# A graph network on one core: extra, unused matrix products in the stage that builds the adjacency tiles

## The chip, the cores and the metric

The kernel runs on one core of one Trainium2 chip. The metric is the device time of that core in microseconds (us): the median of the runs of the kernel before is 6002.23 us, of three runs from 5999.04 to 6010.08 us. Less is better.

## The reference, cut to what matters

The reference is a network of four graph layers on 6250 nodes with 64 features and 200,000 edges, sorted by destination: a two-round gated message layer, a graph convolution, a mean aggregation with edge features, and an edge network followed by a gated unit. The sums over edges that the first three need are all of this kind:

```
msg_in = jnp.concatenate([hv[dst], hv[src], e], axis=1)
msgs = msg_in @ W_msg[t] + b_msg[t]
a = jax.ops.segment_sum(msgs, dst, num_segments=num_nodes)
...
out = jax.ops.segment_sum(msgs, dst, num_segments=n_nodes)      # convolution
agg = jax.ops.segment_sum(x_j, col, num_segments=N)             # mean
```

A sum over edges of rows of the source nodes is a product with the adjacency matrix (how many edges go from source s to destination d). The kernel builds that matrix once and multiplies with it several times. Only the building is touched here.

## The kernel before, in words

**The building.** The 6250 nodes are cut into 49 tiles of 128 (`NT`). A destination tile is cut into 16 windows of 8 destination nodes (`WT`, `DW`). For each window the result is a matrix of 128 (position of the source in its tile) by 392 (49 source tiles by 8 destinations), held in one PSUM bank; four banks are used in turn (`bank_w`: two halves of `ps_zz`, `ps_t`, `ps_a`). The edges lie in chunks of 128, one edge to a partition; since they are sorted by destination, a window needs a run of chunks, taken two at a time (`GW`): a *group*. Each window has a first group and, in a loop, as many *further groups* as its edges need (`more`). The destinations are drawn so that small node numbers have most edges: the first tile has 108 further groups in its 16 windows, the last ones have none.

**Who does what.** For each group VectorE makes two one-hot operands: the position of the source (`oh_lo`, L1555) and the pair of source tile and destination (`oh_hi`, L1557), and then signals `s_wsem`. TensorE waits for it (L1125), multiplies the two chunks' operands into the bank (two MATMULs of 392 columns, L1127) and with the second gives the operand buffer back (`s_woh`). There are four buffers for first groups, one per bank, and two for further groups: `rest = GF + k % 2`, one for even windows and one for odd. So a second further group of a window is written only when TensorE has read the first. When a window's groups are done TensorE closes the bank with a product of one column (L1135), signals `s_win`, and ScalarE copies the bank as fp8 into the tile (L800) and frees it (`s_winf`). After each tile ScalarE makes the keys of the tile after the next one (L789, L790), and SyncE stores the finished tile to DRAM.

**Order.** All order is that in which the code is written; there is no planner. TensorE's loop runs over 49 tiles with 16 windows written out, with a loop over further groups in each. VectorE's and ScalarE's loops take two tiles a turn. At each tile's start TensorE and VectorE load the tile's counts into registers (L421). After the 49 tiles TensorE transposes an auxiliary matrix and goes on to the first product with the adjacency.

**Unused products elsewhere.** The gated units already have such a thing: `WARM = 16` products of `ident_h` with itself, 128 columns each, written into `ps_a` and never read (L997).

Of the kernel before, what the change touches and what calls it, by code (L numbers as in the profile page):

```python
# [22 lines left out]
P = 128  # L23
# [55 lines left out]
def gnn(nc, D, out):  # L79
    with ExitStack() as ctx:  # L80
        def sb(name, shape, dt=f32):
            return ctx.enter_context(nc.sbuf_tensor(name, shape, dt))

        def ps(name, shape):
            return ctx.enter_context(nc.psum_tensor(name, shape, f32))
# [60 lines left out]
        ident_h = sb("ident_h", [P, P], bf16)  # L146
# [118 lines left out]
        ps_acc = ps("ps_acc", [P, 512])  # L265
# [153 lines left out]
        def load_windows(eng, t, first):  # L419

            _, vals = nc.values_load_multi_w_load_instructions(  # L421
                win_tab[0:1, ds(t, 1), first:2, :].rearrange("o t a w -> o (t a w)"), engines=[eng.engine],
                min_val=0, max_val=CH, skip_runtime_bounds_check_because="chunk numbers and counts")
            lim = [(0, CH - 1), (0, GWMAX - 1)][first:]
            vals = [nc.s_assert_within(r, *lim[k // WT], skip_runtime_bounds_check_because="the search bounds it")
                    for k, r in enumerate(vals)]
            return [(k % GF, GF + k % 2, k, *vals[k::WT]) for k in range(WT)]

        def load_range(eng, t, which=(0, 1)):

            lim = [(0, CH - 1), (1, GMAX), (0, NT * GMAX), (1, SMAX), (1, RBMAX), (1, RBG), (0, CH - 1)]
            k0, k1 = which[0], which[-1] + 1
            _, vals = nc.values_load_multi_w_load_instructions(
                tile_tab[0:1, ds(t, 1), k0:k1].rearrange("o w a -> o (w a)"), engines=[eng.engine],
                min_val=0, max_val=NT * GMAX, skip_runtime_bounds_check_because="chunk numbers and counts")
            return [nc.s_assert_within(vals[k - k0], *lim[k], skip_runtime_bounds_check_because="the search bounds it")
                    for k in which]
# [126 lines left out]
        def _(pool):  # L564
# [26 lines left out]
            with pool.Fori(0, NT) as t:  # L591
                lo, _, _, ng = load_range(pool, t, (0, 1, 2, 3))
                with pool.Fori(0, ng) as g:
                    c = first_chunk(pool, lo, g, 2 * SC, CH - 1)
                    for b in range(2):
                        features = e16a[:, ds(c + b * SC, SC), :]
                        pool.wait_ge(s_e3f, 1)
                        pool.sem_inc(s_e3f, -1)
                        pool.tensor_tensor(eparts[:, b, 1, :, :], features, upper(features), ALU.subtract).then_inc(s_pool, 1)  # L599
                        pool.wait_ge(s_pool, 1)  # L600
                        pool.sem_inc(s_pool, -1)
                        pool.tensor_tensor(eparts[:, b, 2, :, :], eparts[:, b, 1, :, :], eparts_h[:, b, 1, :, :],
                                           ALU.subtract).then_inc(s_e3, 1)
# [287 lines left out]
        def _(pe):  # L891
# [223 lines left out]
            def build_tile(t):  # L1115

                if True:
                    for i, rest, _, more in load_windows(pe, t, 1):
                        pe.wait_ge(s_winf[i], 1)
                        pe.sem_inc(s_winf[i], -1)  # L1120

                        def group(first):
                            u = i if first else rest
                            pe.wait_ge(s_wsem, 1)
                            pe.sem_inc(s_wsem, -1)  # L1125
                            for j in range(GW):
                                m = pe.matmul(bank_w[i][:, 0:WC], oh_lo[u][:, :, j], oh_hi[:, u, j, :],  # L1127
                                              start=first and j == 0, stop=False)
                            m.then_inc(s_woh[u], 1)

                        group(True)
                        with pe.If(more):
                            with pe.Fori(0, more):
                                group(False)
                        pe.matmul(bank_w[i][:, 0:1], zrow_h[0:1, 0:P], zrow_h[:, 0:1], start=False,  # L1135
                                  stop=True).then_inc(s_win, 1)


            pe.wait_ge(s_cst2, 1)
            pe.sem_inc(s_cst2, -1)  # L1140
# [33 lines left out]
            for k in range(3):  # L1174
# [3 lines left out]
                          stop=True).then_inc(s_wc, 1)  # L1178
# [4 lines left out]
            with pe.Fori(0, NT) as t:  # L1183
                build_tile(t)
# [756 lines left out]
```

## Time and profile before

| what | value |
| --- | --- |
| median of three runs | 6002.23 us (5999.04 to 6010.08) |
| profiled execution | 5999.94 us, of which the span is 5998.2 us |
| mean granted TensorE clock over the span | 0.717 |
| building the adjacency | 818.7 to 2131.7 us of the span, 1313.0 us |
| in it: TensorE busy | 873.60 us |
| in it: VectorE busy | 745.99 us |
| in it: ScalarE busy | 576.84 us |

"Granted clock" is the mean of TensorE's clock over a stretch as a share of full speed: it has two levels here, 1.0 (2.4 GHz) and 0.5 (1.2 GHz), and a value between them says how much of the stretch was at each. A matrix product's busy time contains the time that it needs to drain, so products that follow each other overlap in it and a busy TensorE is not one at its peak. The three stretches used below are tiles 0 to 4 (818.7 to 1239.2 us), tiles 5 to 27 (to 1778.1 us) and tiles 28 to 48 (to 2131.7 us).

### The profile page before, as it was taken

To read this page: it belongs to the slowest core of one execution; us is meant where nothing else is said; L and a number is where in the kernel's file an instruction comes from. 1 tells how busy PE (TensorE), PEld (TensorE's weight loads), DVE (VectorE), ACT (ScalarE), POOL (GpSimd) and SP (SyncE) were. 2 spreads that over 40 slices of the span, in tenths; PEclk is the share of its full clock that TensorE was granted. 3 is DMA by queue.
4 is the path that set the end of the run, shared out by engine and by line. 5 is a ranking of instruction groups with operands and counts; after the bars stand their busy time and mean duration, and the time that the engine had idled before them with its cause. 6 is when DMAs were issued, how large, how long until landed. Compare 5 with 4: busy or idle time off the path is not lost. (4 is left out here: it accounts for less than half of the span.)

```text
span 5998.2 us, 125746 instructions
## 1 busy us (share of the span) xinstructions
PE 3920.0 (65%) x29847; PEld 2606.8 (43%) x29848; DVE 3033.9 (51%) x8943; ACT 1290.4 (22%) x3582; POOL 2274.8 (38%) x2798
## 2 busy tenths in 40 slices
PE   0455325667677779797998985666666666666666
PEld 0344201122222258787988873333333333333335
DVE  4444753466666555333123225555555555555554
ACT  0222100144556730121000111111111111111112
POOL 0455560000000000211111016777777777777771
PEclk9999755588887789998999995555555555555557
DMA  3000000000001135132544433333333333333330
GB/s 128 0 0 0 1 2 6 11 29 32 39 39 50 50 133 179 44 134 103 176 156 176 140 109 84 91 88 88 89 88 88 88 87 87 87 87 87 86 85 23
DMA packets 220192, 460.12 MB, mean 77 GB/s; under 512 B 59440, under 2 KB 116796, under 8 KB 219357
## 3 DMA queue, kind: packets, MB, share of 16 engines
q1 hardware_dynamic: 163325, 401.37, 19.9%
q0 software_dynamic: 56672, 56.94, 5.3%
q14 instruction: 169, 1.38, 0.1%
q8 instruction: 26, 0.43, 0.0%
HBM read 415.43 MB, written 42.67 MB: 76 GB/s over the span
## 5 line engine op out<-in xcount | busy, mean ns | idle before, releaser
L676 POOL DMA_INDIRECT scr<-ptable,idx_st x1722 | 1668.8, 969 | 589.0 <-issue 439.5
L644 POOL COPY late<-late 128x256 f32<-128x256 f32 (+1 forms) x65 | 25.3, 390 | 2500.5 <-POOLq L642 2500.5
L937 PE MATMUL ps_zz<-sb_w_e,late 64*128 64x128 f32 x1148 | 439.6, 485 | 399.8 <-PEq L936 384.5
L1018 PE MATMUL ps_zz<-scr,arena 128*128 128x192 bf16 x7203 | 616.9, 248 | 65.1 <-PEq L1016 65.1
L1018 PEld LDWEIGHTS ps_zz<-scr,arena 128*128 128x128 fp8e4 x7203 | 605.3, 99 | 75.6 <-issue 72.9
L868 ACT COPY idx_st<-src_i 128x2 int32 x864 | 166.0, 192 | 1921.2 <-ACTq L874 1921.2
L937 PEld LDWEIGHTS ps_zz<-sb_w_e,late 64*128 64x128 f32 x1148 | 286.1, 308 | 577.5 <-issue 573.2
L950 PE MATMUL ps_acc<-scr,onehot 128*128 128x192 bf16 x1722 | 414.1, 341 | 162.8 <-PEq L948 144.7
L1557 DVE TENSOR_TENSOR arena<-arena 128x196 int32 x1323 | 470.2, 355 | 0.2 <-issue 0.2
L1127 PE MATMUL ps_zz<-arena,cand 128*128 128x392 fp8e4 x784 | 249.0, 408 | 337.5 <-PEq L1125 334.5
L1335 DVE TENSOR_TENSOR scr<-scr 128x128 f32<-128x128 f32 x861 | 253.8, 295 | 408.8 <-DVEq L1334 400.5
L1018 PE MATMUL ps_zz<-arena 128*128 128x192 bf16 x4802 | 406.1, 247 | 25.1 <-PEq L1016 25.1
L1018 PEld LDWEIGHTS ps_zz<-arena 128*128 128x128 fp8e4 x4802 | 400.2, 98 | 29.4 <-issue 28.1
L1441 DVE TENSOR_REDUCE arena<-ps_zz 128x64 f32<-128x192 f32 x196 | 70.1, 358 | 636.1 <-DVEq L1439 636.0
L937 PE MATMUL ps_t<-sb_w_e,late 64*128 64x128 f32 x574 | 219.1, 483 | 261.7 <-PEq L936 220.5
L1318 DVE TENSOR_TENSOR onehot<-dst_s,itile 128x256 bf16<-128x256 int16 x861 | 367.5, 427 | 6.2
L1312 DVE TENSOR_SCALAR late<-scr,tcol 128x256 bf16 x861 | 315.8, 367 | 41.5 <-DVEq L1311 31.6
L1327 DVE TENSOR_TENSOR scr<-ps_zz,scr 128x128 f32<-128x128 f32 x574 | 167.0, 291 | 315.9 <-DMA scr<-ptable,idx_st 228.5
L1555 DVE TENSOR_TENSOR scr<-scr,late 128x256 bf16<-128x256 f16 x539 | 157.5, 292 | 312.7 <-DVEq L1554 229.7
L937 PEld LDWEIGHTS ps_t<-sb_w_e,late 64*128 64x128 f32 x574 | 143.1, 308 | 349.5 <-issue 344.5
L940 PE MATMUL ps_zz<-arena,late 128*128 x3444 | 288.2, 240 | 0.0
L599 POOL TENSOR_TENSOR eparts<-arena 128x102 f32 x310 | 160.3, 517 | 325.2 <-DVEq L1700 172.6
(335 smaller groups left out, 5971.0 us busy)
## 6 DMA issues: line engine op xcount, KB each, us to landing
arena<-a_dram SPq DMA_DIRECT2D x245, 784.0 KB, 4.3
scr<-in_dst_lin SPq DMA_DIRECT2D x287, 384.0 KB
a_dram<-arena SPq DMA_DIRECT2D x49, 784.0 KB, 3.3
scr<-ptable,idx_st POOLq DMA_INDIRECT x1722
late<-in_e32c SPq DMA_DIRECT2D x861, 32.0 KB
arena<-in_e16p SPq DMA_DIRECT2D x1, 13387.5 KB, 34.7
h<-mm_dram SPq DMA_DIRECT2D x2, 832.0 KB, 5.3
x<-in_x_nm SPq DMA_DIRECT2D x1, 1664.0 KB, 7.0
```

The source lines that it names most:

```text
L676: pool.indirect_dma_start(grow[:, j, :], None, ptable, bass.IndirectOffsetOnAxis(ap=idx_st[:, j:j + 1], axis=0)).then_inc(s_row[j], 16)
L868: act.copy(idx_st[:, 2 * b:2 * b + 2], src_i[:, ds(c + 2 * b, 2)]).then_inc(s_ix, 1)
L937: pe.matmul(z, e32t[:, b, :], W["w_e3"][:, :], start=True, stop=False).then_inc(s_etf[b], 1)
L940: m = pe.matmul(z[:, i * H:(i + 1) * H], onehotT[:, b, i * P:(i + 1) * P], qsp[:, ds(t, 1), p * H:(p + 1) * H], start=False, stop=i == 1 a ...
L950: m = pe.matmul(ps_acc[:, 0:3 * H], onehot[:, j, :], msg_h[:, j, :, :], start=False, stop=False)
L1018: last = pe.matmul(ps_z[b % 2][:, 0:3 * H], amat[b][:, i, :], hsp[k % 2][:, i, :], start=(i == 0), stop=(i == NT - 1))
L1127: m = pe.matmul(bank_w[i][:, 0:WC], oh_lo[u][:, :, j], oh_hi[:, u, j, :], start=first and j == 0, stop=False)
L1312: v.tensor_scalar(onehotT[:, b, :], dstb[:, ds(r, 1), b, :], tcol[:, ds(t, 1)], None, ALU.is_equal).then_inc(s_ohT, 1)
L1318: v.tensor_tensor(onehot[:, 2 * b:2 * b + 2, :], bc(dst_s[:, ds(c + 2 * b, 2)], P), itile[:, :].unsqueeze(1).broadcast_to([P, 2, P]), ALU. ...
L1327: v.tensor_tensor(pre[:, 2 * b:2 * b + 2, :], bank_z[b][:, 0:2 * H].rearrange("p (j f) -> p j f", j=2), grow[:, 2 * b:2 * b + 2, :], ALU.a ...
L1335: v.tensor_tensor(msg[:, j, 1, :], msg[:, j, 0, :], msg_h[:, j, 0, :], ALU.subtract).then_inc(s_v, 1)
L1557: v.tensor_tensor(oh_hi_i[:, u, :, :, :], src_hot[:, ds(c, GW), :].unsqueeze(3).broadcast_to([P, GW, NT, 2]), dst_word[:, ds(c, GW), :].un ...
```

## The change

Behind each further group TensorE makes one product that nobody reads, and behind each closing of a window two. The product has 384 columns: `ident_h`, a bf16 identity of 128 by 128, times three copies of itself, into the bank `ps_acc`, which nothing else uses in this stage. It waits for nothing and signals nothing. The signals of the further group (`s_woh`) and of the closing (`s_win`) stand on the instructions before it.

```diff
                             m.then_inc(s_woh[u], 1)
+                            if not first:
+                                idle_product()
 
                         group(True)
                         with pe.If(more):
...
                         pe.matmul(bank_w[i][:, 0:1], zrow_h[0:1, 0:P], zrow_h[:, 0:1], start=False,
                                   stop=True).then_inc(s_win, 1)
-
+                        for n in range(2):
+                            idle_product()
+
+            def idle_product():
+                pe.matmul(ps_acc[:, 0:3 * P], ident_h[:, :], ident_h[:, :].unsqueeze(1).broadcast_to([P, 3, P]),
+                          start=True, stop=True)
```

TensorE's instructions for the first window of a tile, and the start of the second, before. `cand` and `scr` are the first and the further group's `oh_lo`, `arena` their `oh_hi`, `zrow_h` the closing's row of zeros; the rows between the branches run once per further group:

```order
L1127 MATMUL ps_zz<-arena,cand 128x392 [waits s_winf0,s_wsem]
L1127 MATMUL ps_zz<-arena,cand 128x392
L1132 COMPARE_AND_BRANCH
L1133 UNCONDITIONAL_BRANCH
L1127 MATMUL ps_zz<-arena,scr 128x392 [waits s_wsem]
L1127 MATMUL ps_zz<-arena,scr 128x392
L1133 REGISTER_ALU
L1133 COMPARE_AND_BRANCH
L1132 UNCONDITIONAL_BRANCH
L1135 MATMUL ps_zz<-zrow_h 128x1
L1127 MATMUL ps_zz<-arena,cand 128x392 [waits s_winf1,s_wsem]
```

The next window's first product follows the closing directly. The same place now:

```order
L1127 MATMUL ps_zz<-arena,cand 128x392 [waits s_winf0,s_wsem]
L1127 MATMUL ps_zz<-arena,cand 128x392
L1134 COMPARE_AND_BRANCH
L1135 UNCONDITIONAL_BRANCH
L1127 MATMUL ps_zz<-arena,scr 128x392 [waits s_wsem]
L1127 MATMUL ps_zz<-arena,scr 128x392
L1143 MATMUL ps_acc<-ident_h 128x384
L1135 REGISTER_ALU
L1135 COMPARE_AND_BRANCH
L1134 UNCONDITIONAL_BRANCH
L1137 MATMUL ps_zz<-zrow_h 128x1
L1143 MATMUL ps_acc<-ident_h 128x384 x2
```

One product has come into the loop over further groups, behind the product that frees the buffer, and two stand between the closing (now L1137) and the next window's first group. On the other engines no instruction moves.

## Rows read from the trace of the kernel before

**Rows 1.** Windows, all engines, the building in three stretches: busy time (instructions), then granted clock.
```profile
core 0: us, PE busy (x) PEld busy (x) DVE busy (x) ACT busy (x) POOL busy (x), PEclk, DMA share, GB/s
818.70:1239.20 420.50, 236.76 (x696) 55.26 (x696) 172.86 (x614) 56.43 (x89) 25.04 (x27) 0.53 0.03 9
1239.20:1778.10 538.90, 376.59 (x1632) 121.85 (x1632) 355.86 (x1264) 275.05 (x414) 0.00 (x0) 0.84 0.09 35
1778.10:2131.70 353.60, 260.25 (x1102) 83.52 (x1102) 217.26 (x769) 245.36 (x378) 0.00 (x0) 0.74 0.12 49
```

**Rows 2.** Windows, the same stretches, only the closings of L1135.
```profile
818.70:1239.20 420.50, 14.28 (x80) 7.75 (x80) 0.53 0.03 9
1239.20:1778.10 538.90, 63.88 (x368) 33.87 (x368) 0.84 0.09 35
1778.10:2131.70 353.60, 58.93 (x336) 31.50 (x336) 0.74 0.12 49
```

**Rows 3.** Timeline, tile 0, a chain of further groups: start, duration, engine, line, idle before.
```profile
1001.16 0.29 DVE L1555 TENSOR_TENSOR scr<-scr,late 128x256 bf16<-128x256 f16 x1 [1.54 <-DVEq L1554]
...
1001.88 0.81 PE L1127 MATMUL ps_zz<-arena,scr 128*128 128x392 fp8e4 x2 [1.08 <-PEq L1125]
1003.05 0.29 DVE L1555 TENSOR_TENSOR scr<-scr,late 128x256 bf16<-128x256 f16 x1 [1.32 <-DVEq L1554]
```

**Rows 4.** Timeline, tile 0, where one window ends and the next begins.
```profile
1010.20 0.18 PE L1135 MATMUL ps_t<-zrow_h 1*128 1x1 bf16 x1
...
1010.31 0.83 PE L1127 MATMUL ps_a<-arena,dif 128*128 128x392 fp8e4 x2
...
1010.94 0.86 PE L1127 MATMUL ps_a<-arena,scr 128*128 128x392 fp8e4 x2
1012.16 0.29 DVE L1555 TENSOR_TENSOR scr<-scr,late 128x256 bf16<-128x256 f16 x1 [1.55 <-DVEq L1554]
```

**Rows 5.** Timeline, tile 38, windows with one group each, low clock.
```profile
1961.62 0.83 PE L1127 MATMUL ps_zz<-arena,cand 128*128 128x392 fp8e4 x2
...
1962.39 0.18 PE L1135 MATMUL ps_zz<-zrow_h 1*128 1x1 bf16 x1
...
1962.50 0.83 PE L1127 MATMUL ps_t<-arena,dif 128*128 128x392 fp8e4 x2
```

**Rows 6.** Timeline, the same tile 8 us later, high clock.
```profile
1970.19 0.51 PE L1127 MATMUL ps_t<-arena,dif 128*128 128x392 fp8e4 x2
...
1970.63 0.17 PE L1135 MATMUL ps_t<-zrow_h 1*128 1x1 bf16 x1
...
1970.73 0.51 PE L1127 MATMUL ps_a<-arena,dif 128*128 128x392 fp8e4 x2
```

**Rows 7.** Line L997: duration min/median/max in ns, first and last start.
```profile
L997 PE MATMUL ps_a<-ident_h x384: 217/219/219, 2401.1 to 5983.6; 128*128 128x128 bf16 x192
```

**Rows 8.** Timeline, the last gated unit, products of L997 and their weight loads.
```profile
5909.70 0.65 PEld L997 LDWEIGHTS ps_a<-ident_h 128*128 128x128 bf16 x9
5909.86 0.61 PE L997 MATMUL ps_a<-ident_h 128*128 128x128 bf16 x8
```

**Rows 9.** Timeline, VectorE at the start of a tile, a first group, a further one, a first one.
```profile
1505.05 0.29 DVE L1555 TENSOR_TENSOR cand<-scr,late 128x256 bf16<-128x256 f16 x1 [2.36 <-DVEq L1554]
...
1505.90 0.29 DVE L1555 TENSOR_TENSOR scr<-scr,late 128x256 bf16<-128x256 f16 x1 [0.29 <-issue]
...
1506.50 0.29 DVE L1555 TENSOR_TENSOR cand<-scr,late 128x256 bf16<-128x256 f16 x1
```

**Rows 10.** Timeline, from the end of tile 37 to the start of tile 38.
```profile
1954.67 0.50 ACT L800 ACTIVATE arena<-ps_a 128x392 fp8e4<-128x392 f32 x1
...
1957.62 2.11 ACT L790 ACTIVATE late<-x,neg_base 128x1663 f16<-128x1663 f32 x1
1960.06 0.29 DVE L1555 TENSOR_TENSOR cand<-scr,late 128x256 bf16<-128x256 f16 x1 [6.26 <-DVEq L1554]
```

**Rows 11.** Windows, the first 3.5 us of TensorE's work in the tile of rows 9.
```profile
1505.70:1509.20 3.50, 3.36 (x11) 0.96 (x12) 2.70 (x10) 3.03 (x3) 0.00 (x0) 0.52 0.39 160
```

## The prediction, made before the change was run

> **What bounds the kernel now.** I read the windows view first, the building cut into three stretches [rows 1]. It is 1313.0 of 5998.2 us, and nothing outside it is touched, so all of the prediction is here. The reader should see that no engine is full: TensorE is busy 56%, 70% and 74% of the three stretches, VectorE 41%, 66% and 61%, ScalarE 13%, 51% and 69%. And TensorE's granted clock is 0.53, 0.84 and 0.74: in the first five tiles it is nearly always at the low level, though TensorE is busy more than half the time.
>
> Then the counts. The closings are 80, 368 and 336 [rows 2], 16 to a tile: 5, 23 and 21 tiles. Taken off the 696, 1632 and 1102 products of [rows 1] they leave 616, 1264 and 766 products of L1127, two to a group: 308, 632 and 383 groups, of which 228, 264 and 47 are further ones. So the change adds 2 x 784 + 539 = 2107 products.
>
> Last the timeline, for what each stretch waits on.
> - *Tiles 0 to 4: a chain through one buffer.* A further group's operands are written at 1001.16, multiplied from 1001.88 to 1002.69, and the next ones are written at 1003.05 [rows 3]: 1.89 us a group at the low clock, with TensorE idle 1.08 us of it.
> - *Tiles 5 to 27: VectorE.* It takes 0.85 us from a first group to a further one and 0.60 us from any group to the next first one [rows 9]. A tile has 16 windows and 264 / 23 = 11.5 further groups: 16 x 0.60 + 11.5 x 0.85 = 19.4 us. At the tile's start it stands 2.36 us [rows 9] or, at its loop's turn every second tile, 6.26 us [rows 10], 4.3 on average. Sum 23.7 us; measured 538.9 / 23 = 23.4. So VectorE's own pace explains this stretch.
> - *Tiles 28 to 48: VectorE and TensorE in turn.* VectorE's sum is 9.6 + 2.2 x 0.85 + 4.3 = 15.8 us a tile, measured 353.6 / 21 = 16.8. TensorE needs 0.88 us a window at the low clock (1961.62 to 1962.50) [rows 5] and 0.54 at the high (1970.19 to 1970.73) [rows 6], so at the low clock it is the slower one.
>
> **What a product costs.** Eight products of 128 columns with the same `ident_h` take 0.61 us, of which the last one's own duration is 0.219 [rows 7, 8]: (0.61 - 0.219) / 7 = 0.056 us each. Three times that is 0.17 us for 384 columns at the high clock. The pair of 392 columns says the same: 0.51 at high against 0.83 at low [rows 5, 6], a difference of 0.32 us in 784 columns, which makes 0.16 us a product at high and 0.33 at low. Two products behind a closing: 0.33 us high, 0.65 us low. Weight loads: nine of them take 0.65 us beside the eight products [rows 8], so they hide behind these; the first, behind the one-column closing, is exposed, but in its place the next window's first load goes behind the second product. A window with one group then costs TensorE 0.54 + 0.33 = 0.87 us at high and 0.88 + 0.65 = 1.53 at low, against VectorE's 0.60.
>
> The product behind a further group falls in the 1.08 us of idle time of [rows 3]: nobody waits. Cost 0 in a chain, and 0.16 us where TensorE is the bound. If the idle time were gone it would cost 0.16 to 0.33.
>
> **Tiles 0 to 4: +18 us.** At a window's turn the closing is at 1010.20, the first group at 1010.31, the further one at 1010.94, and VectorE goes on at 1012.16 when that one has been read [rows 4]. The two products stand between the first two of these, on the path: 80 x 0.65 = +52 us if the clock stays low. If it were always high they would cost 80 x 0.33 = 26, and the path would win back 0.32 us (0.83 against 0.51) in each of the 228 further groups, 73 us, and again in up to 80 first groups, 26: net -73. Those are the bounds. Between them decides how much of the time the clock is high. Now it is 6% (0.53). The products fill the turns of windows: 2 + 4 products of the groups + 1 in one piece, then the chain again with gaps of 0.7 us. The first tile has 108 further groups, in long chains where one product a group leaves TensorE idle for a third of the time; I expect the low clock there. In tiles 1 to 4, with one to three further groups a window, I expect high clock for half the time or more. Together some 33% high, 27 points more than now: 52 - 0.27 x 125 = +18.
>
> **Tiles 5 to 27: +17 us.** TensorE at the high clock: 16 x 0.87 + 11.5 x (0.33 + 0.16) = 19.5 us a tile. Its head is added. After tile 37's last closing ScalarE copies the bank at 1954.67, then makes keys until 1957.62 + 2.11 = 1959.73, and only then can it copy the next tile's first bank, 0.5 us [rows 10]: free at 5.9 us after the closing (0.3 us before the copy). TensorE fills four banks in 4 x 0.87 = 3.5 us and waits 2.4. Where VectorE's stand is 6.26 instead, its lead of four buffers covers 3.5 of it, which leaves about the same, 2.8. After such a pause the clock is low for a while, as now (0.52 in the first 3.5 us of a tile, after 2.36 us of standing) [rows 9, 11]: in 3.5 us two windows at 1.53 in place of 0.87, 1.3 to 2 us. Head 4.1 us; sum 23.6, as much as VectorE's 23.7. The mean is a tie, but the tiles differ. With 17 further groups VectorE's sum is 28.4 and TensorE's 26.3, no loss. With 5 they are 18.1 and 20.5: +2.4. Over the 23 tiles I take +0.75 a tile, +17. Bounds: 0, and +2.4 x 23 = +55.
>
> **Tiles 28 to 48: +47 us.** 13.9 + 2.2 x 0.49 + 4.1 = 19.1 us a tile on TensorE against 16.8 now: +2.25 x 21 = +47. Bounds: without the low clock after the head, 17.4, +13; with a head of 6 us, +87.
>
> **Sum.** 18 + 17 + 47 = +82 us. Against the profiled execution, 5999.94 us (span 5998.2 and 1.7 around it), that is 6082; the median of the runs is 2 us above the profiled one, so 6084 us, 1.4% slower. Where does the gain go? The clock rises in all three stretches, to about 0.65, 0.93 and 0.9, but only the first one waits for TensorE enough to be paid for it.
>
> **Rivals.**
> - *The clock pays (faster).* Products make the clock high throughout tiles 0 to 4 and at the tiles' heads. The place is the chain of [rows 3]; its price is up to -73 us, of which I take -45, since turns with one further group go at VectorE's 0.85 + 0.60 whatever the clock; then 0 in the middle and +11 late: about 5968 us. It decides once more than 42% of the first stretch's path is high (52 / 125) and the tile's head costs no low clock. For it: the added products raise TensorE's work in a chain by half. Against it: a chain even at high keeps TensorE idle for most of its 1.57 us, and today 0.56 busy [rows 1] gives 0.53 of clock. The Trainium skill, "TensorE: Matmul & The Clock Gate" (table "Why this matters for your kernels"), says that a matmul stream stays at full clock unless it has a long idle gap. By that rule this rival would hold. The trace disagrees: gaps of 1.08 us, and the low clock. Chance 0.06.
> - *The products are hidden (no change).* All three stretches have idle TensorE time, 183.7, 162.3 and 93.4 us [rows 1]. If the turns could absorb 784 x 0.33 = 259 us, the time stays at 6002. Against it: the late stretch has 93 us idle, and 336 x 0.33 = 111 go in. Chance 0.05.
> - *Products of an identity do not lift the clock (much slower).* Then real work is a smaller share of each stretch and the clock falls to low throughout: late 21 x (16 x 1.53 + 2.2 x 0.98 + 2.4) - 354 = +255; middle 23 x (24.5 + 11.5 x 0.98 + 2.4) - 539 = +339; early +52: 6650 us. No row separates it: L997's products stand among others. Chance 0.04.
> - *Each product's weight load is exposed.* 0.1 us more for each of two products in the windows where TensorE is the bound, the 336 late ones and half of the middle: 520 x 0.2 = +104, 6188 us. The Trainium skill, the same page (Part 2, the step on getting the stationary operand), lets the queue pull a load ahead of products in flight, which is this rival's denial; the trace agrees for L997 [rows 8], but not for the closing, 0.77 us after its group's start at the low clock where the two products need 0.65 [rows 5]. Chance 0.05.
>
> **How the numbers follow.** My forecast has 0.80. Its own range is 6035 to 6130: the early term from -15 to +45, the middle 0 to +35, the late +30 to +65, not all at one end. To leave out no more than 2 in 10 the range goes a little further, towards the exposed loads above and the clock that pays below: 6028 to 6140. A measurement of this kernel tells about 0.2%, 12 us, from no change. Slower by more: 0.80 less a little, + 0.04 + 0.05 = 0.88; the same 0.05; faster 0.07.
>
> **What would show it.** In the changed profile the building should end about 82 us later, with the late stretch some 19 us a tile, TensorE's idle time there ended by the free bank once a tile, and successive windows 0.87 us apart. The chain of tile 0 should keep 1.89 us at the low clock, and its turns be 0.65 us longer. The product's duration should follow 0.16 us start to start. Granted clock of about 0.65, 0.93, 0.9. If tile 0 shows a high clock, my early term is wrong and the sum falls; if late windows are 1.07 us apart, the loads are exposed; if the clock is 0.5 in all, products of an identity do not count.

## The result, and the profile after

The changed kernel takes 6078.76 us (median of four runs, 6074.57 to 6080.44) against 6000.64 us for the kernel before in the same comparison: a ratio of 1.0126, with a 95% interval from 1.0108 to 1.0143. The prediction was 6084 us, 82 us or 1.4% slower. Measured once more, beside the experiments of "Both, and the change once more" below, the ratio was 1.0134 (1.0118 to 1.0149).

The windows view of the changed kernel, the building in the same three stretches of tiles (0 to 4, 5 to 27, 28 to 48); columns as in [rows 1], then tile 0 and tiles 1 to 4 apart:

```profile
core 0: us, PE busy (x) PEld busy (x) DVE busy (x) ACT busy (x) POOL busy (x), PEclk, DMA share, GB/s
817.70:1249.30 431.60, 292.77 (x1084) 101.68 (x1084) 172.87 (x614) 56.37 (x89) 24.93 (x27) 0.68 0.03 8
1249.30:1814.50 565.20, 485.91 (x2633) 222.33 (x2632) 355.97 (x1264) 273.87 (x415) 0.00 (x0) 0.93 0.08 34
1814.50:2214.00 399.50, 342.50 (x1822) 150.62 (x1822) 217.64 (x770) 243.64 (x377) 0.00 (x0) 0.91 0.11 43
...
818.70:1026.00 207.30, 134.45 (x402) 40.42 (x400) 68.79 (x244) 7.75 (x16) 24.23 (x26) 0.57 0.01 1
1026.00:1249.30 223.30, 157.31 (x682) 61.03 (x680) 103.51 (x368) 47.99 (x73) 0.00 (x0) 0.79 0.04 15
```

The building ends at 2214 us in place of 2132 and everything behind it is as long as before. The stretches are +11, +26 and +46 us longer, and the clock rose in each: from 0.53 to 0.68, from 0.84 to 0.93, from 0.74 to 0.91. The clock did what such products can do, and the kernel got slower all the same. VectorE's busy time has not moved (172.87, 355.97, 217.64).

The line of the added product: count, and the shortest, median and longest duration in ns.

```profile
L1143 PE MATMUL ps_acc<-ident_h x2107: 323/326/528, 819.0 to 2213.9; 128*128 128x384 bf16 x192
```

It is the 2107 that were counted. What they do to successive windows stands in the timeline of tile 41, each window with one group, at the high clock:

```profile
2080.47 0.50 PE L1127 MATMUL ps_zz<-arena,cand 128*128 128x392 fp8e4 x2
...
2080.90 0.17 PE L1137 MATMUL ps_zz<-zrow_h 1*128 1x1 bf16 x1
2081.00 0.50 PE L1143 MATMUL ps_acc<-ident_h 128*128 128x384 bf16 x2
...
2081.23 0.29 DVE L1562 TENSOR_TENSOR cand<-scr,late 128x256 bf16<-128x256 f16 x1 [0.30 <-DVEq L1561]
2081.34 0.50 PE L1127 MATMUL ps_zz<-arena,cand 128*128 128x392 fp8e4 x2
```

Group, closing, two products, next group: 0.87 us, where [rows 6] had 0.54. TensorE's rows have no idle time before them: it waits for nobody. VectorE now waits for it: before its next first group it stands 0.30 us at L1561, where it waits for an operand buffer to be read. Over the late stretch its waits there before first groups grew from 110.5 to 161.9 us (the waits view of `cand` and `dif`). In tile 0 the turn of a window and the chains around it, with the start of VectorE's next operand:

```profile
1001.60 0.29 DVE L1562 TENSOR_TENSOR scr<-scr,late 128x256 bf16<-128x256 f16 x1 [1.32 <-DVEq L1561]
1002.31 0.81 PE L1127 MATMUL ps_zz<-arena,scr 128*128 128x392 fp8e4 x2 [0.76 <-PEq L1125]
1002.91 0.53 PE L1143 MATMUL ps_acc<-ident_h 128*128 128x384 bf16 x1
1003.49 0.29 DVE L1562 TENSOR_TENSOR scr<-scr,late 128x256 bf16<-128x256 f16 x1 [1.32 <-DVEq L1561]
...
1004.20 0.81 PE L1127 MATMUL ps_zz<-arena,scr 128*128 128x392 fp8e4 x2 [0.76 <-PEq L1125]
...
1004.81 0.52 PE L1143 MATMUL ps_acc<-ident_h 128*128 128x384 bf16 x1
1005.26 0.18 PE L1137 MATMUL ps_zz<-zrow_h 1*128 1x1 bf16 x1
1005.38 0.82 PE L1143 MATMUL ps_acc<-ident_h 128*128 128x384 bf16 x2
1005.99 0.86 PE L1127 MATMUL ps_zz<-arena,cand 128*128 128x392 fp8e4 x2
...
1007.87 0.29 DVE L1562 TENSOR_TENSOR scr<-scr,late 128x256 bf16<-128x256 f16 x1 [2.50 <-DVEq L1561]
1008.58 0.49 PE L1127 MATMUL ps_zz<-arena,scr 128*128 128x392 fp8e4 x2 [0.88 <-PEq L1125]
...
1009.44 0.29 DVE L1562 TENSOR_TENSOR scr<-scr,late 128x256 bf16<-128x256 f16 x1 [1.00 <-DVEq L1561]
```

The chain of [rows 3] still takes 1.89 us (1001.60 to 1003.49) with the product inside it: TensorE's idle time fell from 1.08 to 0.76 us, and the chain is no longer for it. The turn costs: from the last further group to the closing 1.06 us (1004.20 to 1005.26), from there to the next group 0.73 (to 1005.99) where [rows 4] had 0.11. Then, after the dense turn, the clock is high, and the next chain takes 1.57 us (1007.87 to 1009.44).

### The profile page after: what moved, and what is told of

The parts are those of the page before. It is cut to its first block and busy times, and to the rows that moved or that the text cites. A ratio compares the mean times of both kernels' runs of the same rounds, so it can differ in the third digit from the quotient of the medians.

```text
span 6078.6 us, 129960 instructions
## 1 busy us (share of the span) xinstructions
PE 4170.9 (69%) x31954; PEld 2821.8 (46%) x31955; DVE 3031.2 (50%) x8943; ACT 1287.2 (21%) x3582; POOL 2272.1 (37%) x2798
## 5 line engine op out<-in xcount | busy, mean ns | idle before, releaser
L1143 PE MATMUL ps_acc<-ident_h 128*128 128x384 bf16 x2107 | 621.2, 357 | 0.0
L1127 PE MATMUL ps_zz<-arena,cand 128*128 128x392 fp8e4 x784 | 216.6, 361 | 279.6 <-PEq L1125 279.6
```

The source lines that it names most:

```text
L1143: pe.matmul(ps_acc[:, 0:3 * P], ident_h[:, :], ident_h[:, :].unsqueeze(1).broadcast_to([P, 3, P]), start=True, stop=True)
```

## The experiments

All comparisons are with the kernel before on the same chip in the same call. Two things must be known to read them. The first four (each place alone, one column, three in chains) ran on one chip, on which the kernel before takes 6732 us, and the next three (tile ends, both, keys in the middle) on another, with 6739 us. On both the part behind the building is some 700 us longer and tile 0 some 25 us (see the last section); the other tiles of the building are as in the first comparison. I call these two the slower chips. The last four runs are from a third chip, where the kernel before takes 6005 us, about as in the first comparison (6001 us); which chip that one ran on is not on record. And the last stretch of the kernel before is 353.6 us in one profile and 359.9 in another [rows 1, and below], so a few us there say nothing. The three stretches of an experiment are given as its windows rows have them; the kernel before was not profiled on the slower chips, so as its first stretch there I take the 446 us of the run that leaves that stretch nearly alone (products at tile ends only). The times in us that go with a ratio are the ratio's difference from 1 times the kernel before.

### Each of the two places alone

```diff
-                        for n in range(2):
-                            idle_product()
```

> Only the product behind each further group stays, the two behind a closing go. Theory A (a product costs what it puts on TensorE's path, and the clock pays little): the product behind a window's last further group stands before the closing and the next first group, so the turns of tiles 0 to 4 get 0.33 us longer (26 us), the clock pays some of it back; the later tiles are VectorE's again. +5 to +20 us on before, late stretch within 3 us of the 353.6 before. Rival B (my prediction's sentence that a product in a chain costs nothing): 0, or faster by what the clock gives. Rival C (both kinds cost in proportion to their columns, 539 of 2107 products): +20 us.

Measured: ratio 1.0007 (0.9991 to 1.0024). Stretches 443.4, 545.0, 359.4 us, granted clock 0.64, 0.87, 0.76. So -3, +6 and 0 to +6: no change that can be told, -6 to +16 us by the interval, which holds rival B and most of theory A. The clock of the first stretch rose from 0.53 to 0.64 and paid little more than the turns took.

```diff
-                            if not first:
-                                idle_product()
```

> Only the two products behind each closing stay. Theory A: all of the late loss and most of the rest stays, +75 to +90 us on before: in tiles 28 to 48 TensorE still needs 0.87 us a window, in tiles 0 to 4 the turns still take 0.65 us more at the low clock, and the chains, without a product of their own, get less of the high clock than in the change (granted clock of the first stretch below 0.65), so the first stretch is longer than the 430.6 us of the change. Rival C (in proportion to columns, 1568 of 2107): +60 us.

Measured: ratio 1.0074 (1.0046 to 1.0102), 31 to 69 us. Windows view:

```profile
818.80:1271.70 452.90, 247.79 (x856) 72.72 (x856) 173.41 (x614) 56.36 (x89) 24.81 (x27) 0.64 0.02 8
1271.70:1827.20 555.50, 460.90 (x2369) 195.18 (x2368) 356.13 (x1264) 274.99 (x415) 0.00 (x0) 0.90 0.08 34
1827.20:2221.50 394.30, 335.32 (x1776) 146.10 (x1776) 217.81 (x770) 243.94 (x377) 0.00 (x0) 0.92 0.11 44
```

Against 446, 539 and 354 to 360 that is +7, +16 and +34 to +41. Most of the loss is that of the products behind the closings, and nearly all of the late one (394.3 of 399.5 us). The total is lower than the +75 to +90 that I expected. By the stretches the two places alone come to some 65 us against 80 of both, by the intervals to anything from 25 to 85, so whether they do more together than apart stays open.

### Instructions without columns

```diff
-                pe.matmul(ps_acc[:, 0:3 * P], ident_h[:, :], ident_h[:, :].unsqueeze(1).broadcast_to([P, 3, P]),
+                pe.matmul(ps_acc[:, 0:1], ident_h[:, :], ident_h[:, 0:1],
```

> The change with its products cut to one column: the same number of instructions and weight loads, no streaming. Theory A, where the clock follows the columns that are streamed and not the number of instructions: the clock falls below that of before, towards 0.5 in all three stretches, because each product's weight load (0.1 us) is now exposed and spreads the real columns out. TensorE then needs 0.88 + 0.21 = 1.1 us a window at the low clock: 21 x (17.6 + 3) late is +75, +50 to +100 in the middle, +30 early; +150 to +210 us. Rival D (instructions or weight loads keep the clock up, streaming is not needed): the clock stays as in the change, a window costs 0.54 + 0.2 = 0.75 us at high, under VectorE's pace at most tiles, and the kernel lands between before and +30 us.

Measured: ratio 1.0016 (0.9998 to 1.0034), -1 to +23 us. Windows view:

```profile
818.70:1268.00 449.30, 243.63 (x1084) 93.96 (x1084) 173.38 (x614) 56.33 (x89) 24.74 (x27) 0.53 0.02 8
1268.00:1810.10 542.10, 392.06 (x2632) 171.89 (x2632) 356.09 (x1264) 275.19 (x415) 0.00 (x0) 0.84 0.09 35
1810.10:2175.40 365.30, 287.07 (x1823) 108.75 (x1824) 217.79 (x770) 244.75 (x377) 0.00 (x0) 0.71 0.12 48
```

Its timeline, a late window with one group at the high clock:

```profile
1965.29 0.49 PE L1127 MATMUL ps_a<-arena,dif 128*128 128x392 fp8e4 x2
1965.72 0.17 PE L1137 MATMUL ps_a<-zrow_h 1*128 1x1 bf16 x1
1965.82 0.20 PE L1143 MATMUL ps_acc<-ident_h 128*128 128x1 bf16 x2
1965.88 0.49 PE L1127 MATMUL ps_zz<-arena,cand 128*128 128x392 fp8e4 x2
```

The same 2107 instructions and weight loads, and the clock is that of before: 0.53 and 0.84, and 0.71 in the late stretch, where the kernel before has 0.74 in one profile and 0.70 in another. So the instructions and loads alone do not raise it; with their 384 columns they do. Theory A had that right and the time wrong (+150 to +210 us, at a clock below that of before); the time is inside rival D's range, but D's clock, that of the change, is not there. I had each load cost 0.1 us; here a window takes 0.59 us (1965.29 to 1965.88) against 0.54 before, so two products with their loads cost 0.05 us once they have no columns. The late stretch is 5 to 12 us longer, and of the change's +46 the columns are the rest. With that the rival of the exposed weight loads is out.

### Where products cost nothing

```diff
                         with pe.If(more):
-                            with pe.Fori(0, more):
-                                group(False)
+                            with pe.If(pe.snap(more - 1)):
+                                with pe.Fori(1, more):
+                                    group(False)
+                                    for n in range(3):
+                                        idle_product()
+                            group(False)
```

> No product behind closings nor behind the last further group of a window; three behind each further group that another one follows (148 of them, where TensorE stands 1.08 us). Theory A: nothing is put on the path of a turn, three products take 0.99 us at the low clock and 0.5 at the high, both inside the 1.08 us, and the clock rises in tiles 0 to 4: chains at 1.57 in place of 1.89 us. First stretch 365 to 385 us in place of 420.5, the other two unchanged: -35 to -58 us on before. Rival E (what the further groups lose is their wait for VectorE, the clock cannot shorten the chain): 0. Rival F (three products reach into the next group's start): slower, a chain above 1.89 us.

Measured: ratio 0.9924 (0.9902 to 0.9946), -36 to -66 us. Windows view:

```profile
818.30:1215.40 397.10, 241.09 (x1140) 91.63 (x1140) 173.11 (x614) 56.31 (x89) 24.86 (x27) 0.92 0.03 9
1215.40:1755.80 540.40, 375.84 (x1635) 122.15 (x1635) 356.12 (x1264) 275.33 (x415) 0.00 (x0) 0.85 0.09 35
1755.80:2116.10 360.30, 272.49 (x1104) 84.04 (x1105) 217.79 (x770) 245.25 (x377) 0.00 (x0) 0.70 0.12 48
```

The first stretch is 49 us shorter than the 446 of the slower chips, at a clock of 0.92, and the other two are as before. A step of the chain takes 1.57 us, as expected (in tile 0 VectorE's operands follow each other at 905.67, 907.23), so rivals E and F are out. 444 more products where nobody waits for TensorE pay; fewer products than the change has (444 against 2107).

The same place with one product a group, as in the change (`range(1)`, the only difference), ran on the third chip:

> One product behind each further group that another one follows, as in the change, none elsewhere: what the change's own product does in a chain when nothing lies on the turns. Theory A: it hides (0) and lifts the clock little: chains of tile 0 keep 1.89 us and the low clock, first stretch within 10 us of before, total within 10 us of before. Rival L (one product in a chain is enough, and the turns hid it in the change): -30 us or more, as with three.

Measured: ratio 0.9995 (0.9986 to 1.0004). Its first stretch:

```profile
817.60:1237.30 419.70, 281.09 (x844) 77.03 (x844) 172.81 (x614) 56.35 (x89) 24.97 (x27) 0.54 0.02 9
```

The kernel before has 419.8 us at 0.53 on this chip. One product hides and lifts nothing. The rewritten loop is the same in both runs, so it is the two further products that pay in the run before. In tiles 1 to 4 the clock is 0.58 here, but 0.77 where every further group has its product, the last of a window too, and 0.76 where only the closings have theirs. So in the change the rise in these tiles (to 0.79) came from the turns, and products on the turns are what had to be paid for.

### The tile ends

Eight products behind a tile's sixteenth window, none elsewhere:

```diff
+                    for n in range(8):
+                        idle_product()
```

> Eight products behind a tile's last closing, none elsewhere. They fall in TensorE's stand at a tile's head (2.4 us in odd tiles, 6.2 in even ones), need 1.3 us at the high clock and 2.6 at the low. Theory A: nobody waits for them, and a tile's first windows are at the high clock more often; the late tiles, where TensorE at the low clock is the slower engine, gain: granted clock of the last stretch from 0.74 to 0.8 or more, -8 to -20 us on before. Rival G (the low clock after a head is hidden behind VectorE anyway): 0. Rival H (they hold back the next tile's first group in odd tiles): up to 49 x 0.3 = +15 us.

Measured: ratio 0.999 (0.9976 to 1.0003). The clock rose as expected, 0.93 and 0.86 in the second and third stretch, which are 539.6 and 352.1 us long: 0 and -2 to -8 us. By the interval the whole may be anything from -16 to +2 us, so this run does not show a gain. In the middle stretch this is rival G: the low clock after a head is hidden behind VectorE.

### Both, and the change once more

Three in chains and eight at tile ends together, first on the slower chip of the tile ends:

> Three products in chains and eight at tile ends. Theory A: the two gains add: -50 to -73 us on before, first stretch 365 to 385 us, last one 340 to 348. Rival: only the better of the two shows.

Measured: ratio 0.9904 (0.9886 to 0.9923), -52 to -77 us; stretches 396.6, 539.6 and 348.7 us. By the stretches the two gains add (397.1 and 352.1 us each alone); by the ratios they may as well not, since the intervals overlap. Then on the third chip, beside the change and a profile of the kernel before:

> The change as it is, beside the kernel before and the next runs on one chip, since the other experiments ran on a chip on which the kernel before takes 6732 us. Theory A: the building gets some 80 us longer whatever the rest takes: +70 to +85 us. Rival K (on a chip whose DMA is slower the loss is partly hidden): under +60 us, as the closings' products alone gave +50.

> The kernel before, profiled on the chip of the other runs of this call: the building's three stretches at 420 to 446, 539 and 353 us.

> Three products behind each further group that another follows, eight behind a tile's last closing, once more, beside the kernel before and the change on one chip. Theory A: the building 60 to 70 us shorter than before, 1.0 to 1.1% of the whole.

The change: 1.0134 (1.0118 to 1.0149), +81 us by medians. Chains and ends: 0.9898 (0.9883 to 0.9913), 5943.48 us against 6004.99. Windows view of the kernel before, and of chains and ends:

```profile
817.30:1237.10 419.80, 237.54 (x696) 55.42 (x696) 172.82 (x614) 56.36 (x89) 24.89 (x27) 0.53 0.02 9
1237.10:1776.50 539.40, 376.67 (x1632) 121.84 (x1632) 355.79 (x1264) 275.24 (x415) 0.00 (x0) 0.84 0.09 35
1776.50:2136.40 359.90, 274.65 (x1104) 84.25 (x1105) 217.52 (x770) 245.20 (x377) 0.00 (x0) 0.70 0.12 48
```

```profile
817.30:1184.40 367.10, 242.54 (x1175) 93.89 (x1176) 172.85 (x614) 56.37 (x89) 24.95 (x27) 0.98 0.03 10
1184.40:1723.40 539.00, 393.79 (x1820) 135.53 (x1819) 355.80 (x1264) 274.76 (x415) 0.00 (x0) 0.94 0.09 35
1723.40:2070.40 347.00, 267.93 (x1272) 96.22 (x1270) 217.22 (x768) 243.97 (x377) 0.00 (x0) 0.89 0.12 50
```

At a clock of 0.98 the first stretch is 53 us shorter. At 0.94 in place of 0.84 the middle is as long as before to half a us: VectorE's pace explains its length, and TensorE's clock is worth nothing there. The late stretch gains 7 to 13 us. This version beats both kernels.

### The head of a tile

The change, with ScalarE's keys made in the middle of a tile's copies:

```diff
                 for w in range(WT):
+                    if w == WT // 2 and keys is not None:
+                        tile_keys(*keys)
...
-                tile_keys(i * 2 + 1, 1)
-                build_tile(0)
-                tile_keys(i * 2 + 2, 0)
-                build_tile(1)
+                build_tile(0, (i * 2 + 1, 1))
+                build_tile(1, (i * 2 + 2, 0))
```

> The change, with ScalarE making the next tile's keys after eight of a tile's sixteen banks and not before the first. Theory A (in the change TensorE stands at every second tile's head for a free bank, 1.6 us in the profile): the stand at L1120 goes and the late stretch falls from 399.6 us by 10 x 1.6 = 16 or more, the total to +60 to +70 us on before. Rival I (the stand at the head is VectorE's register loads and loop turn, whatever ScalarE does): no change against the change, +78. Rival J (4.3 us of keys in the middle of a tile make TensorE stand for a bank there): slower than the change.

Measured: ratio 1.0085 (1.0061 to 1.0109), +41 to +73 us, which holds theory A's +60 to +70; rival I's +78 is just outside. Its last stretch:

```profile
1846.30:2221.60 375.30, 329.92 (x1823) 146.84 (x1822) 217.88 (x770) 236.03 (x377) 0.00 (x0) 0.98 0.11 46
```

375.3 us against 399.5 of the change, at a clock of 0.98 in place of 0.91: what ScalarE does at the head counts, and rival I is out. The wait of 1.6 us ahead of a tile's fifth window is gone, and the one ahead of every second tile's first product is mostly 1.1 to 2.5 us in place of 3.5 to 4.7. In ten tiles a new one of 1.4 us stands some twelve windows in, four behind the keys: that is rival J's wait, and it is the smaller. Together TensorE's waits at L1125 in this stretch fell from 56.9 to 44.5 us, half of the 24; the rest goes with the clock. The middle stretch is 4 us longer than in the change (568.9), which this run does not explain.

## Why the prediction was right, point by point

- **What a product costs, 0.16 us at the high clock, with its load hidden.** Right: a late window takes 0.87 us as forecast, and in the one-column run the same loads with hardly any columns cost 0.05 us of it.
- **Tiles 28 to 48, +47 us.** Measured +46 (399.5 against 353.6; +40 against the second profile's 359.9), 19.0 us a tile where 19.1 was forecast. The mechanism is right; that the number fits so closely is in part luck, since the parts of the tile's head were mis-sized and made it up together. The changed kernel's tile 37, four windows in, and start of tile 42:

```profile
2000.82 0.49 PE L1127 MATMUL ps_zz<-arena,cand 128*128 128x392 fp8e4 x2 [1.66 <-PEq L1125]
...
2091.22 0.29 DVE L1562 TENSOR_TENSOR cand<-scr,late 128x256 bf16<-128x256 f16 x1 [6.78 <-DVEq L1561]
2091.93 0.81 PE L1127 MATMUL ps_zz<-arena,cand 128*128 128x392 fp8e4 x2 [4.33 <-PEq L1125]
```

  The wait for a free bank was to be 2.4 us and is 1.66 (ahead of a tile's fifth window). The other, in every second tile, was to be 2.8 us of VectorE's stand and is 4.33: VectorE stands 6.78 us, and its lead covered 2.45 of that (6.78 - 4.33) and not the 3.5 that four buffers would give. And the low clock comes nearly only behind the longer wait, where the forecast had it in every tile: behind the 1.66 us the pair takes 0.49 us, behind the 4.33 us 0.81.
- **Tiles 5 to 27, +17 us.** Measured +26 (565.2 against 538.9). Right in kind; the 0.75 us a tile that I took between 0 and 2.4 was too small by half (26 / 23 = 1.1). The closings' products alone made +16 of it and the further groups' alone +6. Tiles that I had without loss do lose: counted from a tile's first product to the next tile's, tiles 6, 8 and 10, with 16 further groups each, got 0.7 to 1.0 us longer, and nearly all of the stretch's loss is in the even tiles (20.8 us became 22.6 on average, the odd ones' 26.2 became 26.7).
- **Tiles 0 to 4, +18 us.** Measured +11. The turn's 0.65 us came as forecast (0.62). One term was missed: "the product behind a further group costs 0 in a chain" is right for a chain, as the run with one product there shows, but behind a window's *last* further group it stands before the closing: 1.06 us where it was 0.75, 0.3 us in each of 80 turns, 24 us. The clock's share came as forecast (0.68 for 0.65), and tile 0 stayed low (0.57). So the sum with the missed term should have been near +38 us. What brought it down to +11 is that the products cost little where the clock is high: from tile 2's first product to tile 5's the change takes 130.6 us at 0.95 (133.6 when measured again), and the version with no product on a turn 126.6 at 0.96. That is 4 to 7 us for 48 turns, where 0.87 - 0.54 + 0.16 = 0.49 us each would make 24. VectorE's own pace, which one of the prediction's rivals named, is the likely cover; no run tests it. Against the kernel before, these three tiles are 8 us shorter (5 when measured again) and tiles 0 and 1 together 20 us longer (17). The two errors have opposite signs, and that the sum is only 7 us off is luck.
- **The rivals.** "The products are hidden" and "products of an identity do not lift the clock" are out by the first profile. "The clock pays" is half right: three products in a chain raise the first stretch's clock to 0.92 and pay 49 us (0.98 and 53 us on the third chip, with products at the tile ends as well), one pays nothing. The prediction said that this rival would hold by the rule that it quoted from the Trainium skill ("TensorE: Matmul & The Clock Gate", the table of its last part), by which only a long idle gap costs the full clock, and it called the low clock of [rows 3] a disagreement. Those rows alone do not show one, since TensorE had not been at the high clock in that stretch before (it is 0.50 all the way from 819 to 1181 us). Tile 0 of the changed kernel does:

```profile
1010.15 0.50 PE L1127 MATMUL ps_zz<-arena,scr 128*128 128x392 fp8e4 x2 [0.92 <-PEq L1125]
1010.48 0.33 PE L1143 MATMUL ps_acc<-ident_h 128*128 128x384 bf16 x1
1010.74 0.17 PE L1137 MATMUL ps_zz<-zrow_h 1*128 1x1 bf16 x1
1010.85 0.82 PE L1143 MATMUL ps_acc<-ident_h 128*128 128x384 bf16 x2
```

  The clock was high (0.50 and 0.33 us) and fell (0.82 us for two products that take 0.50 at the high clock), with no idle time of TensorE above 0.92 us since it had risen. So here a full clock was lost without a long gap, and the rule does not hold in this kernel.

## What to carry to other kernels

A product that nobody reads is free only where TensorE waits for another engine and where no next product is queued behind it; ask of each place what instruction comes next and who waits for that. The granted clock is no measure of success: it rose in all three stretches here, the middle one did not gain from TensorE's speed at all and the late one by 7 to 13 us at most. Put such products inside the longest dependent chain, enough of them, and leave the turns alone: 444 there and 392 at tile ends gave -1.0%, where 2107 everywhere gave +1.3%.

## What the runs showed of the hardware that I had not expected

On the two slower chips VectorE nearly stood still at the start of tile 0, while GpSimd issued the last 25 of its 49 indirect gathers (0.94 us each). The timeline of the run with products at tile ends:

```profile
835.70 0.29 DVE L1562 TENSOR_TENSOR scr<-scr,late 128x256 bf16<-128x256 f16 x1 [5.95 <-issue]
...
837.10 0.41 DVE L1564 TENSOR_TENSOR arena<-arena 128x196 int32 x1 [1.11 <-issue]
...
844.09 0.29 DVE L1562 TENSOR_TENSOR scr<-scr,late 128x256 bf16<-128x256 f16 x1 [6.58 <-issue]
```

It waited for nothing that the profile shows, 4.6 to 6.6 us before each of four groups, of which two are shown. In the first comparison and on the third chip the same instructions and gathers have no such gap: the windows view of 820 to 850 us, first of the kernel before in the first comparison, then of the run with products at tile ends on its slower chip, has 33 products of TensorE against 12, with GpSimd the same.

```profile
820.00:850.00 30.00, 12.80 (x33) 2.18 (x32) 9.04 (x32) 0.00 (x0) 22.69 (x25) 0.50 0.08 7
```

```profile
820.00:850.00 30.00, 4.67 (x12) 0.68 (x10) 3.15 (x10) 0.00 (x0) 22.68 (x25) 0.50 0.08 7
```

What VectorE waited for is open. A second surprise is how little a weight load costs when it follows another: two products of one column, loads and all, make a window 0.05 us longer (0.59 for 0.54).
